# Cross-attentions of a twelve-layer kernel: flips handed over bank by bank, the output projection in the bank of the attended values, plain turns

## The chip, the cores and the metric

The kernel runs on one core of one Trainium2 chip, as one program that computes all twelve layers. The metric is the device time of a whole execution, in microseconds (us); lower is better.

## The reference, cut to what matters

The input `x` is 32 batches of 64 tokens with 256 channels. Twelve layers are added to it one after the other. Layers L0x, L2x and L3x are cross-attentions of 16 heads of 16 channels over 256 context tokens per batch:

```python
def _L0_xattn_ref(query, key, value, Wq, bq, Wk, bk, Wv, bv, Wo, bo):
    B, S, D, H = (4, 512, 256, 16)
    HD = D // H
    b = query.shape[0]
    Q = (query @ Wq + bq).reshape(b, -1, H, HD).transpose(0, 2, 1, 3)
    K = (key @ Wk + bk).reshape(b, -1, H, HD).transpose(0, 2, 1, 3)
    V = (value @ Wv + bv).reshape(b, -1, H, HD).transpose(0, 2, 1, 3)
    energy = jnp.einsum('bhqd,bhkd->bhqk', Q, K) / np.sqrt(HD)
    attn = jax.nn.softmax(energy, axis=-1)
    x = jnp.einsum('bhqk,bhkd->bhqd', attn, V)
    x = x.transpose(0, 2, 1, 3).reshape(b, -1, H * HD)
    return x @ Wo + bo
...
x = x + _L0_xattn_ref(_layernorm(x, axis=-1), ctx_1024, ctx_1024, ...)
```

L3x adds `mask * -1e9` to the scores. L2x has no projections at all: the normed `x` is the query, the context is key and value, and nothing is multiplied behind the attention. L0f is a layer whose two expert matrices are mixed anew for each of the 64 positions out of eight experts and then applied (`W1 = einsum('be,eoi->boi', g, eW1)`, a ReLU, and the same with `eW2`).

## The kernel before, in words

The three cross-attentions share `cross_attention` (line 739). `OWN` is true in L0x and L3x, where keys, values and output are projected, and false in L2x. Each engine runs its own list of instructions, written out by hand in a loop over the 32 batches `b`, and the engines meet by semaphores. The order of work on TensorE (PE) per batch is:

- `flip(b, 0)` (L924): eight transposes of the probabilities of the first half of the head pairs into `psT`, two PSUM banks. `PR` holds the probabilities, `PT` the transposed ones.
- `project_keys(b + 2)` (only OWN, L75 to L77 by way of `three_passes`) into the bank `psA`.
- `scores(b + 1, ...)` (L908, with a mask L912 too) into `psS`, four banks: both halves at once in the OWN layers, one half here and one half later in L2x.
- `flip(b, 1)`: eight more transposes into the same two banks.
- every second batch `finish(b // 2 - 1)`: the output projection of the last 128 tokens (L955), or in L2x two transposes (L957), into `psA`.
- in L2x the second half of the scores; in the OWN layers `project_values(b + 1)` into `psA`.
- `attend(b)`: two matmuls with `TWO`, the sum of two identities (L932), which turn the spread inverse sums `RB` around and add their two halves, into columns 128 to 255 of `psO`; then 32 matmuls (L944) of the probabilities with the values into columns 0 to 127 of `psO`.

ScalarE (ACT) takes the exponentials of a half (`exponentiate`, four ACTIVATEs with accumulation, L1001), copies bank 0 of `psT` to `PT` (`turned`, L1007), and in the OWN layers adds the key bias (`keys`, L1012) and rounds the context to its high part (`high`, L1019). Its order is `turned(b,0)`, `keys(b+2)`, `turned(b,1)`, both halves of `exponentiate(b+1)`, `high(b+4)`.

VectorE (DVE) takes the maxima (`largest`, L1044, 1,024 elements each), copies bank 1 of `psT` (`turned`, L1049), inverts the sums (`invert`, L1065), copies the values out of `psA` (`values`, L1053), scales the attended values (`attended`, L1071 and L1073), makes the low part of the context (`low`, L1058), and every second batch adds the projected output to `x` (`finish`, L1077). `turned(b,1)`, `finish`, `largest(b+1,1)`, `values(b+1)`, `attended(b)` follow one another in that order. GpSimd (POOL) spreads queries and inverse sums.

Two rules tie PE to the others. `psT` is handed over whole: `flip` waits until both copies of the flip before are done (`s_ta`, `s_td`), and signals once, behind its eighth transpose. And `psA` is shared: `FILLS` lists its users in order (K keys, W output projection, V values), and `claim` makes each wait until the one before has been read out (`s_empty`).

In L0f, `position_experts` (line 1700) runs 16 steps `k`. Its jobs go alternately to two sets of four PSUM banks, `S[0]` and `S[1]`, and `claim` makes a job wait until the job two places before it has been read out, by ACT, by DVE or by both. f0 to f3 and g0 to g3 are mixings (`mix2`, L1836, and `mix1`, L1823), which both engines read out; A0 and A1 apply the first mixed matrix (`apply1`, L1852 and L1859) and are read out by one ACT instruction; T turns the weights of the next block (L1810).

## Time and profile before

| what | value |
|---|---|
| median of three runs | 3020.52 us (3018.69 to 3025.06) |
| the profiled execution's own time | 3015.32 us |
| its span, first to last instruction | 3013.5 us |
| busy: PE, DVE, ACT, POOL | 86%, 60%, 45%, 21% |
| mean granted TensorE clock | 0.926 |
| batch loop of L0x | 59 to 322 us |
| 16 steps of L0f | 498 to 858 us |
| batch loop of L2x | 2036 to 2234 us |
| batch loop of L3x | 2531 to 2820 us |

The profile follows one execution. PE is matmul work, PEld the loading of the stationary operand, which runs ahead of the matmuls; of both, the start times are the best guide, since ends are modelled. A figure in square brackets behind a row is idle time of the engine just before it, with the instruction that ended it; "issue" is idle time for which the profile shows no releaser. A waiting share says little by itself: each loop has to be read for what closes it.

### The profile page before, as it was taken

What the parts mean: (1) busy time and instruction counts of PE and PEld (TensorE: products, weight loads), DVE (VectorE), ACT (ScalarE), POOL (GpSimd) and SP (SyncE); (2) the same over time, 40 slices, a digit from 0 to 9 for tenths busy, and PEclk for the clock granted to TensorE, in tenths of its full rate; (3) what the DMA queues carried; (4) which work ended last, traced back from release to release, by engine and by line L of the source; (5) the groups of instructions that cost most, each with busy time, mean ns of one, the idle gap of its engine ahead of it and who ended that gap; (6) DMA issues with size and microseconds to landing.
All of it is one profiled execution on the core that took longest, in us unless ns stands there. A gap on an engine that the chain in (4) does not pass through costs nothing. (4 is left out here: it accounts for less than half of the span.)

```text
span 3013.5 us, 83899 instructions
## 1 busy us (share of the span) xinstructions
PE 2583.9 (86%) x36083; PEld 2146.2 (71%) x36083; DVE 1794.8 (60%) x3365; ACT 1360.9 (45%) x3399; POOL 630.2 (21%) x752
## 2 busy tenths in 40 slices
PE   6999787999958999999987739959986767999888
PEld 5888555777747888888875539957764646888567
DVE  5777675666656444444445645657765866666663
ACT  3777324455532334444331314527763344666441
POOL 3111002211103111111102133422321423222200
PEclk9999898999979999999998559978998788999999
DMA  2110003211031000000000042332220001111100
GB/s 75 34 33 20 16 0 91 58 31 58 3 99 56 2 16 16 16 16 16 2 23 2 3 147 96 118 117 75 89 87 0 2 2 55 44 44 46 43 1 29
DMA packets 118221, 126.67 MB, mean 42 GB/s; under 512 B 10877, under 2 KB 110152, under 8 KB 117864
## 3 DMA queue, kind: packets, MB, share of 16 engines
q1 hardware_dynamic: 114024, 110.93, 11.8%
q0 software_dynamic: 3840, 10.49, 1.1%
q8 instruction: 284, 4.65, 0.6%
q14 instruction: 73, 0.60, 0.1%
HBM read 105.67 MB, written 15.73 MB: 40 GB/s over the span
## 5 line engine op out<-in xcount | busy, mean ns | idle before, releaser
L1001 ACT ACTIVATE s_ca_probs<-s_ca_scores,s_ca_neg_max 128x256 f32<-128x256 f32 x768 | 353.9, 483 | 12.8 <-DVE s_ca_neg_max L1044 9.8
L1044 DVE TENSOR_REDUCE s_ca_neg_max<-s_ca_scores 128x4 f32<-128x1024 f32 x192 | 234.2, 1221 | 103.5 <-PE s_ca_scores L912 54.4
L924 PE MATMUL s_ca_probs_flipped<-identity,s_ca_probs 128*128 128x128 f32 x1536 | 212.6, 282 | 16.0 <-ACT s_ca_probs L1001 9.8
L1375 DVE RECIPROCAL s_cc_inv_sums<-s_cc_sums 128x512 f32<-128x512 f32 x32 | 107.4, 3357 | 182.5 <-PE s_cc_out L1275 182.5
L924 PEld LDWEIGHTS s_ca_probs_flipped<-identity,s_ca_probs 128*128 128x128 f32 x1536 | 167.6, 143 | 59.0 <-ACT s_ca_probs L1001 26.7
L1989 DVE COPY s_mx_w_mixed<-s_mx_ps 128x512 f32<-128x512 f32 x256 | 163.7, 684 | 58.9 <-PE s_mx_ps L1836 43.6
L1007 ACT COPY s_ca_probsT<-s_ca_probs_flipped 128x512 f32<-128x512 f32 x192 | 114.9, 598 | 172.9 <-PE s_ca_probs_flipped L924 172.9
L1944 ACT COPY s_mx_w_mixed<-s_mx_ps 128x512 f32<-128x512 f32 x256 | 137.5, 589 | 114.0 <-PE s_mx_ps L1823 95.1
L1195 POOL TENSOR_TENSOR s_cc_probs_of_both<-s_cc_probsT 128x1024 f32<-128x1024 f32 x32 | 76.8, 2401 | 520.7 <-DVE s_cc_probsT L1366 520.7
L838 POOL TENSOR_TENSOR s_ca_inv_spread<-s_ca_inv_sums,h_ca_own_half 128x128 f32<-128x128 f32 x192 | 72.8, 401 | 473.7 <-DVE s_ca_inv_sums L1065 473.7
L1001 ACT ACTIVATION_READ_ACCUMULATOR s_ca_probs<-s_ca_scores,s_ca_neg_max 128x1 f32 x768 | 164.6, 214 | 0.0
L604 PE MATMUL s_ln_flip<-identity,s_ln_xn 128*128 128x128 f32 x352 | 65.4, 372 | 108.7 <-DVE s_ln_xn L586 108.5
L75 PE MATMUL s_cc_shared<-s_cc_ctxT_low,h_cc_wkv_high 128*128 128x256 f32 x512 | 147.9, 289 | 7.2 <-ACT s_cc_v L1337 3.8
L76 PE MATMUL s_cc_shared<-s_cc_ctxT_high,h_cc_wkv_low 128*128 128x256 f32 x512 | 144.6, 282 | 0.0
L77 PE MATMUL s_cc_shared<-s_cc_ctxT_high,h_cc_wkv_high 128*128 128x256 f32 x512 | 144.5, 282 | 0.0
L1049 DVE COPY s_ca_probsT<-s_ca_probs_flipped 128x512 f32<-128x512 f32 x192 | 131.4, 684 | 21.0 <-PE s_ca_probs_flipped L924 20.2
L604 PEld LDWEIGHTS s_ln_flip<-identity,s_ln_xn 128*128 128x128 f32 x352 | 62.1, 199 | 113.4 <-DVE s_ln_xn L586 112.4
L1327 ACT COPY s_cc_kT<-s_cc_shared 128x512 f32<-128x512 f32 x128 | 75.2, 587 | 90.0 <-PE s_cc_shared L77 88.8
L944 PE MATMUL s_ca_out<-s_ca_probsT,h_ca_v_spread 128*32 128x64 f32 x6144 | 106.5, 221 | 1.3 <-DVE s_ca_probsT L1049 1.3
L75 PEld LDWEIGHTS s_cc_shared<-s_cc_ctxT_low,h_cc_wkv_high 128*128 128x128 f32 x512 | 97.2, 190 | 14.6 <-ACT s_cc_v L1337 7.6
L75 PE MATMUL s_cc_shared<-h_cc_wkv_low,s_cc_ctxT_high 128*128 128x512 f32 x256 | 104.5, 408 | 1.7 <-issue 1.7
L1331 ACT ACTIVATE s_cc_probsT<-s_cc_scores 128x1024 f32<-128x1024 f32 x64 | 63.6, 1026 | 88.9 <-PE s_cc_scores L1257 88.5
(488 smaller groups left out, 7284.8 us busy)
## 6 DMA issues: line engine op xcount, KB each, us to landing
h_ca_ctxT<-in_ctxT SPq DMA_DIRECT2D x96, 256.0 KB, 3.2
h_mx_w_by_input<-in_L_ffn_eW1T SPq DMA_DIRECT2D x16, 512.0 KB, 5.1
h_mx_w_by_hidden<-in_L_ffn_eW2T SPq DMA_DIRECT2D x8, 1024.0 KB, 6.2
h_re_win<-in_L_ffn_W_in SPq DMA_DIRECT2D x8, 1024.0 KB, 5.9
h_ca_ctx<-in_ctx SPq DMA_DIRECT2D x32, 256.0 KB, 2.8
x_normed_transposed<-in_ctx SPq DMA_DIRECT2D x7, 1024.0 KB, 5.5
h_re_wout<-in_L_ffn_W_out SPq DMA_DIRECT2D x8, 512.0 KB, 3.8
choice_results<-s_rt_zeros SPq DMA_DIRECT2D x4, 1024.0 KB, 10.5
```

Of the source, the lines that this page charges most:

```text
L75: nc.tensor.matmul(dst, lhs[0], rhs[1], start=start, stop=False)
L76: nc.tensor.matmul(dst, lhs[1], rhs[0], start=False, stop=False)
L77: return nc.tensor.matmul(dst, lhs[0], rhs[0], start=False, stop=stop)
L604: last = nc.tensor.transpose(flip[u % 4][:, c, k, :], XN[:, t, c * P:(c + 1) * P], ident[:, :])
L924: last = nc.tensor.transpose(psT[:, 2 * a + c, :], PR[b % 2][:, 4 * n + a, c * P:(c + 1) * P], ident[:, :])
L1001: last = nc.scalar.activation(PR[b % 2][:, p, :], psS[:, p // 2, (p % 2) * NKEY:(p % 2 + 1) * NKEY], ACT.Exp, bias=nmax[b % 2][:, p:p + 1] ...
L1007: nc.scalar.copy(PT[b % 2][:, 4 * n:4 * n + 2, :, :].rearrange("p a c q -> p (a c) q"), psT[:, 0:4, :]).then_inc(s_ta, 1)
L1044: nc.vector.tensor_reduce(nmax[b % 2][:, 4 * n:4 * n + 4], psS[:, 2 * n:2 * n + 2, :].rearrange("p r (g k) -> p r g k", g=GR), AX_X, ALU.m ...
L1049: nc.vector.tensor_copy(PT[b % 2][:, 4 * n + 2:4 * n + 4, :, :].rearrange("p a c q -> p (a c) q"), psT[:, 4:8, :]).then_inc(s_td, 1)
L1375: nc.vector.reciprocal(RD[:, :, :], psD[:, :, :]).then_inc(s_rd, 1)
L1944: last = nc.scalar.copy(part(int(name[1]), r), bank(j, r))
L1989: last = nc.vector.tensor_copy(part(int(name[1]), r), bank(j, r))
```

## The change

- **Flips by bank.** `psT` becomes a list of separate banks, two in the OWN layers and three in L2x. Each flip is made of two groups of four transposes; group `u` goes to bank `u % len(psT)`, waits only until that bank's last reader has emptied it, and signals by itself. Even groups are read by ACT, odd ones by DVE. L2x gets its third bank because `psA` no longer exists there.
- **Output projection beside the attended values.** `finish` writes columns 128 to 383 of `psO` (`psW`) and no longer takes part in `FILLS`. So `project_values` doesn't wait for DVE to add the output to `x`; `attend` waits for it instead (`s_we`), every second batch.
- **Plain turns.** The two matmuls with `TWO` become two 128 x 128 transposes with the identity into columns 128 to 383 of `psO`, and the DVE copy of 128 columns becomes a reduction over pairs out of 256 columns. `TWO` and the instruction that made it go.
- **L0f.** A0 goes ahead of f1 on all three engines that handle it.

```diff
--- before.py
+++ after.py
@@ -749,11 +749,8 @@
     for b in range(NB):
...
-        if b and b % 2 == 0:
-            FILLS.append(("W", b // 2 - 1))
...
-    FILLS.append(("W", TILES - 1))
...
@@ -781,16 +777,18 @@
-        psT = ps("ca_probs_flipped", [P, 8, P])
-        psA = ps("ca_shared", [P, 512])
+        psT = [ps("ca_probs_flipped", [P, 4, P]) for _ in range(2 if OWN else 3)]
+        psA = ps("ca_shared", [P, 512]) if OWN else None
...
-        psA2 = psA[:, :].rearrange("p (a b) -> p a b", a=2)
+        psA2 = psA[:, :].rearrange("p (a b) -> p a b", a=2) if OWN else None
+        psW = psO[:, P:P + DIM]
...
+        s_wf, s_we = sem("output_ready"), sem("x_updated")
...
@@ -914,23 +912,27 @@
                 def flip(b, n):
-                    k = 2 * b + n
-                    pe.wait_ge(s_e, k + 1)
-                    if k:
-                        pe.wait_ge(s_ta, k)
-                        pe.wait_ge(s_td, k)
-                    for a in range(4):
-                        for c in range(2):
-                            last = nc.tensor.transpose(psT[:, 2 * a + c, :], PR[b % 2][:, 4 * n + a, c * P:(c + 1) * P], ident[:, :])
-                    last.then_inc(s_t, 1)
+                    pe.wait_ge(s_e, 2 * b + n + 1)
+                    for h in range(2):
+                        u = 4 * b + 2 * n + h
+                        was = u - len(psT)
+                        if was >= 0:
+                            pe.wait_ge(s_td if was % 2 else s_ta, was // 2 + 1)
+                        for a in range(2):
+                            for c in range(2):
+                                last = nc.tensor.transpose(psT[u % len(psT)][:, 2 * a + c, :],
+                                                           PR[b % 2][:, 4 * n + 2 * h + a, c * P:(c + 1) * P], ident[:, :])
+                        last.then_inc(s_t, 1)
...
                 def attend(b):
...
+                    if b and b % 2 == 0:
+                        pe.wait_ge(s_we, b // 2)
                     for g in range(GR):
-                        nc.tensor.matmul(psO[:, P + g * SEQ:P + (g + 1) * SEQ], RB[b % 2][:, g, :, :, :].rearrange("p r h d -> p (r h d)"),
-                                         TWO[:, :], start=True, stop=True)
+                        nc.tensor.transpose(psO[:, P + g * P:P + (g + 1) * P], RB[b % 2][:, g, :, :, :].rearrange("p r h d -> p (r h d)"),
+                                            ident[:, :])
...
@@ -948,14 +950,13 @@
                 def finish(i):
-                    claim(("W", i))
...
                     for g in range(GR):
...
-                            last = nc.tensor.matmul(psA[:, 0:DIM], AT[i % 2][:, g, :], WO[:, g, :], start=(g == 0), stop=(g == GR - 1))
+                            last = nc.tensor.matmul(psW, AT[i % 2][:, g, :], WO[:, g, :], start=(g == 0), stop=(g == GR - 1))
...
-                            last = nc.tensor.transpose(psA[:, g * P:(g + 1) * P], AT[i % 2][:, g, :], ident[:, :])
-                    last.then_inc(s_fill, 1)
+                            last = nc.tensor.transpose(psW[:, g * P:(g + 1) * P], AT[i % 2][:, g, :], ident[:, :])
+                    last.then_inc(s_wf, 1)
...
@@ -1003,8 +1002,9 @@
                 def turned(b, n):
-                    act.wait_ge(s_t, 2 * b + n + 1)
-                    nc.scalar.copy(PT[b % 2][:, 4 * n:4 * n + 2, :, :].rearrange("p a c q -> p (a c) q"), psT[:, 0:4, :]).then_inc(s_ta, 1)
+                    u = 4 * b + 2 * n
+                    act.wait_ge(s_t, u + 1)
+                    nc.scalar.copy(PT[b % 2][:, 4 * n:4 * n + 2, :, :].rearrange("p a c q -> p (a c) q"), psT[u % len(psT)][:, :, :]).then_inc(s_ta, 1)
...
@@ -1045,8 +1045,9 @@
                 def turned(b, n):
-                    dve.wait_ge(s_t, 2 * b + n + 1)
-                    nc.vector.tensor_copy(PT[b % 2][:, 4 * n + 2:4 * n + 4, :, :].rearrange("p a c q -> p (a c) q"), psT[:, 4:8, :]).then_inc(s_td, 1)
+                    u = 4 * b + 2 * n + 1
+                    dve.wait_ge(s_t, u + 1)
+                    nc.vector.tensor_copy(PT[b % 2][:, 4 * n + 2:4 * n + 4, :, :].rearrange("p a c q -> p (a c) q"), psT[u % len(psT)][:, :, :]).then_inc(s_td, 1)
...
@@ -1067,23 +1068,22 @@
                 def attended(b):
...
-                    halves = psO[:, 0:2 * P].rearrange("p (k g q) -> p k g q", k=2, g=GR)
-                    nc.vector.tensor_copy(RT[:, :, :], halves[:, 1]).then_inc(s_rt, 1)
+                    nc.vector.tensor_reduce(RT[:, :, :], psO[:, P:3 * P].rearrange("p (g h q) -> p g q h", g=GR, h=2), AX_X,
+                                            ALU.add).then_inc(s_rt, 1)
...
-                    nc.vector.tensor_tensor(at, halves[:, 0], RT[:, :, :], ALU.mult).then_inc(s_at, 1)
+                    nc.vector.tensor_tensor(at, psO[:, 0:P].rearrange("p (g q) -> p g q", g=GR), RT[:, :, :], ALU.mult).then_inc(s_at, 1)
...
                 def finish(i):
-                    dve.wait_ge(s_fill, PLACE[("W", i)] + 1)
-                    nc.vector.tensor_tensor(X[:, i, :], psA[:, 0:DIM], X[:, i, :], ALU.add).then_inc(s_empty, 1)
+                    dve.wait_ge(s_wf, i + 1)
+                    nc.vector.tensor_tensor(X[:, i, :], psW, X[:, i, :], ALU.add).then_inc(s_we, 1)
...
                 def statistics(i):
-                    dve.wait_ge(s_empty, PLACE[("W", i)] + 1)
+                    dve.wait_ge(s_we, i + 1)
...
@@ -1709,7 +1709,7 @@
-    ORDER = ("f0", "f1", "A0", "T", "f2", "A1", "f3", "FL", "g0", "Y0", "g1", "Y1", "g2", "g3")
+    ORDER = ("f0", "A0", "f1", "T", "f2", "A1", "f3", "FL", "g0", "Y0", "g1", "Y1", "g2", "g3")
...
@@ -1892,8 +1892,8 @@
                 for k in range(NK):
...
+                    apply1(k, 0)
...
-                    apply1(k, 0)
...
@@ -1960,8 +1960,8 @@
                 for k in range(NK):
...
+                    hidden(k, 0)
...
-                    hidden(k, 0)
```

PE in L0x, a batch with an output projection, from the scores to the start of the values; before:

```order
L908 MATMUL s_ca_scores<-s_ca_kT,s_ca_q_spread 128x256 [waits s4_probs_ready_1,s2_ln_normed_1,s2_ln_flipped_1]
L908 MATMUL s_ca_scores<-s_ca_kT,s_ca_q_spread 128x256 x7
L924 MATMUL s_ca_probs_flipped<-identity,s_ca_probs 128x128 [waits s4_probsT_by_dve_1,s4_probsT_by_act_1,s4_probs_ready_1]
L924 MATMUL s_ca_probs_flipped<-identity,s_ca_probs 128x128 x7
L955 MATMUL s_ca_shared<-h_ca_wo,s_ca_attendedT 128x256 [waits s4_attendedT_ready_1,s2_ln_normed_1]
L955 MATMUL s_ca_shared<-h_ca_wo,s_ca_attendedT 128x256
L75 MATMUL s_ca_shared<-h_ca_wkv_low,h_ca_ctxT_high 128x256 [waits s2_ln_normed_1]
L76 MATMUL s_ca_shared<-h_ca_wkv_high,h_ca_ctxT_low 128x256
```

and after the change:

```order
L906 MATMUL s_ca_scores<-s_ca_kT,s_ca_q_spread 128x256 [waits s4_probs_ready_1,s2_ln_normed_1,s2_ln_first_root_taken_1]
L906 MATMUL s_ca_scores<-s_ca_kT,s_ca_q_spread 128x256 x7
L923 MATMUL s_ca_probs_flipped<-identity,s_ca_probs 128x128 [waits s4_probsT_by_act_1,s4_probs_ready_1]
L923 MATMUL s_ca_probs_flipped<-identity,s_ca_probs 128x128 x3
L923 MATMUL s_ca_probs_flipped<-identity,s_ca_probs 128x128 [waits s4_probsT_by_dve_1]
L923 MATMUL s_ca_probs_flipped<-identity,s_ca_probs 128x128 x3
L956 MATMUL s_ca_out<-h_ca_wo,s_ca_attendedT 128x256 [waits s4_attendedT_ready_1]
L956 MATMUL s_ca_out<-h_ca_wo,s_ca_attendedT 128x256
L75 MATMUL s_ca_shared<-h_ca_wkv_low,h_ca_ctxT_high 128x256 [waits s2_ln_normed_1]
L76 MATMUL s_ca_shared<-h_ca_wkv_high,h_ca_ctxT_low 128x256
```

The flip is cut in two groups with one wait on each copying engine, and the output projection has moved from the shared bank to `s_ca_out` and lost its wait on the bank; the wait of the values ahead of L75 now is for the keys' readout alone.

PE in L2x (no projections), a batch with `finish`, from the second flip to the turns of the inverse sums; before:

```order
L924 MATMUL s_ca_probs_flipped<-identity,s_ca_probs 128x128 [waits s21_probsT_by_dve_2,s21_probsT_by_act_2,s21_probs_ready_2]
L924 MATMUL s_ca_probs_flipped<-identity,s_ca_probs 128x128 x7
L957 MATMUL s_ca_shared<-identity,s_ca_attendedT 128x128 [waits s21_attendedT_ready_5,s19_choices5_loaded_1]
L957 MATMUL s_ca_shared<-identity,s_ca_attendedT 128x128
L908 MATMUL s_ca_scores<-h_ca_ctxT,s_ca_q_spread 128x256 [waits s21_probs_ready_2,s16_rstds_ready_1,s19_choices6_loaded_1]
L908 MATMUL s_ca_scores<-h_ca_ctxT,s_ca_q_spread 128x256 x3
L932 MATMUL s_ca_out<-s_ca_two_identities,s_ca_inv_spread 128x64 [waits s21_attendedT_ready_5,s21_inv_sums_spread_2]
L932 MATMUL s_ca_out<-s_ca_two_identities,s_ca_inv_spread 128x64
L944 MATMUL s_ca_out<-s_ca_probsT,h_ca_v_spread 32x64 [waits s21_probsT_by_dve_2,s21_probsT_by_act_2,s17_ln_stored_6]
L944 MATMUL s_ca_out<-s_ca_probsT,h_ca_v_spread 32x64 x31
```

and after (the name of a semaphore in brackets is that of its first user, since semaphores are reused):

```order
L923 MATMUL s_ca_probs_flipped<-identity,s_ca_probs 128x128 [waits s21_probsT_by_dve_2,s21_probs_ready_2]
L923 MATMUL s_ca_probs_flipped<-identity,s_ca_probs 128x128 x3
L923 MATMUL s_ca_probs_flipped<-identity,s_ca_probs 128x128 [waits s21_probsT_by_act_2]
L923 MATMUL s_ca_probs_flipped<-identity,s_ca_probs 128x128 x3
L958 MATMUL s_ca_out<-identity,s_ca_attendedT 128x128 [waits s21_attendedT_ready_5]
L958 MATMUL s_ca_out<-identity,s_ca_attendedT 128x128
L906 MATMUL s_ca_scores<-h_ca_ctxT,s_ca_q_spread 128x256 [waits s21_probs_ready_2,s16_attendedT_ready_4,s19_x_updated_5]
L906 MATMUL s_ca_scores<-h_ca_ctxT,s_ca_q_spread 128x256 x3
L934 MATMUL s_ca_out<-identity,s_ca_inv_spread 128x128 [waits s19_choices7_loaded_1,s21_attendedT_ready_5,s21_inv_sums_spread_2]
L934 MATMUL s_ca_out<-identity,s_ca_inv_spread 128x128
```

The second flip's first group waits for DVE's last copy and the exponentials, its second group for ACT's copy; the turns carry a new wait, that for the update of `x` (shown under a reused name).

PE in L0f, from the last mixing of `g` to the turning of the next weights; before:

```order
L1836 MATMUL s_mx_ps<-me_gate_blocks,s_mx_w_2 128x128 [waits s2_ln_flipped_1,s2_ln_stored_1]
L1836 MATMUL s_mx_ps<-me_gate_blocks,s_mx_w_2 128x128 x15
L1836 MATMUL s_mx_ps<-me_gate_blocks,s_mx_w_2 128x128 [waits s2_ln_stored_1,s2_ln_flipped_1]
L1836 MATMUL s_mx_ps<-me_gate_blocks,s_mx_w_2 128x128 x15
L1852 MATMUL s_mx_ps<-h_mx_b_1,me_gate_rows 128x128 [waits s2_ln_flipped_1,s2_ln_stored_1]
L1852 MATMUL s_mx_ps<-h_mx_b_1,me_gate_rows 128x128 x3
L1859 MATMUL s_mx_ps<-s_mx_w_mixed,x_normed_transposed 32x128 x32
L1810 MATMUL s_mx_ps<-identity,h_mx_w_expert_last 128x128 [waits s2_ln_scales_ready_1,s2_ln_stored_1,s2_ln_flipped_1]
L1810 MATMUL s_mx_ps<-identity,h_mx_w_expert_last 128x128 x15
L1836 MATMUL s_mx_ps<-me_gate_blocks,s_mx_w_2 128x128 [waits s2_ln_flipped_1]
```

and after:

```order
L1823 MATMUL s_mx_ps<-me_gate_blocks,s_mx_w_1 128x128 [waits s2_ln_stored_1]
L1823 MATMUL s_mx_ps<-me_gate_blocks,s_mx_w_1 128x128 x15
L1836 MATMUL s_mx_ps<-me_gate_blocks,s_mx_w_2 128x128 [waits s2_ln_flipped_1,s2_ln_stored_1]
L1836 MATMUL s_mx_ps<-me_gate_blocks,s_mx_w_2 128x128 x15
L1852 MATMUL s_mx_ps<-h_mx_b_1,me_gate_rows 128x128 [waits s2_ln_flipped_1,s2_ln_stored_1]
L1852 MATMUL s_mx_ps<-h_mx_b_1,me_gate_rows 128x128 x3
L1859 MATMUL s_mx_ps<-s_mx_w_mixed,x_normed_transposed 32x128 x32
L1836 MATMUL s_mx_ps<-me_gate_blocks,s_mx_w_2 128x128 [waits s2_ln_stored_1,s2_ln_flipped_1]
L1836 MATMUL s_mx_ps<-me_gate_blocks,s_mx_w_2 128x128 x15
L1810 MATMUL s_mx_ps<-identity,h_mx_w_expert_last 128x128 [waits s2_ln_scales_ready_1,s2_ln_flipped_1]
```

A0 (L1852, L1859) has moved ahead of the second L1836 job, and the turning now waits for what A0 filled.

## Rows read from the trace of the kernel before

**Rows 1.** The page, part 1: busy time, share, instructions.

```profile
PE 2583.9 (86%) x36083; PEld 2146.2 (71%) x36083; DVE 1794.8 (60%) x3365; ACT 1360.9 (45%) x3399; POOL 630.2 (21%) x752
```

**Rows 2.** Waits of PEld, L0x (first) and L3x: total us, times, longest.

```profile
PEld s_ca_shared L75 <- DVE x_resident L1077: 13.9, 15, 1.0
...
PEld s_ca_shared L75 <- DVE x_resident L1077: 13.8, 15, 1.0
```

**Rows 3.** Timeline of L0x, PEld: start, length, engine, line, operation, idle before.

```profile
150.60 0.85 PEld L924 LDWEIGHTS s_ca_probs_flipped<-identity,s_ca_probs 128*128 128x128 f32 x8
...
158.00 0.86 PEld L924 LDWEIGHTS s_ca_probs_flipped<-identity,s_ca_probs 128*128 128x128 f32 x8
...
161.53 0.86 PEld L924 LDWEIGHTS s_ca_probs_flipped<-identity,s_ca_probs 128*128 128x128 f32 x8 [0.33 <-issue]
...
162.35 0.73 PEld L955 LDWEIGHTS s_ca_shared<-h_ca_wo,s_ca_attendedT 128*128 128x128 f32 x4
...
165.43 0.54 PEld L932 LDWEIGHTS s_ca_out<-s_ca_two_identities,s_ca_inv_spread 128*128 128x128 f32 x4
...
166.03 0.94 PEld L944 LDWEIGHTS s_ca_out<-s_ca_probsT,h_ca_v_spread 128*32 128x32 f32 x64
```

**Rows 4.** Timeline of L0x, ACT, DVE and the values' first load.

```profile
155.74 0.48 ACT L1001 ACTIVATE s_ca_probs<-s_ca_scores,s_ca_neg_max 128x256 f32<-128x256 f32 x1
...
159.35 0.67 ACT L1019 CAST h_ca_ctxT_high<-h_ca_ctxT 128x512 fp32r<-128x512 f32 x1
...
161.67 1.23 DVE L1044 TENSOR_REDUCE s_ca_neg_max<-s_ca_scores 128x4 f32<-128x1024 f32 x1 [0.22 <-PE s_ca_scores L908]
...
163.53 0.42 DVE L1077 TENSOR_TENSOR x_resident<-s_ca_shared,x_resident 128x256 f32<-128x256 f32 x1
...
164.01 0.19 PEld L75 LDWEIGHTS s_ca_shared<-h_ca_wkv_low,h_ca_ctxT_high 128*128 128x128 f32 x1 [0.92 <-DVE x_resident L1077]
```

**Rows 5.** Timeline of L2x: PEld, DVE and ACT around two batches.

```profile
2101.42 0.52 PEld L932 LDWEIGHTS s_ca_out<-s_ca_two_identities,s_ca_inv_spread 128*128 128x128 f32 x4 [0.33 <-issue]
...
2106.10 0.25 PEld L957 LDWEIGHTS s_ca_shared<-identity,s_ca_attendedT 128*128 128x128 f32 x2
...
2106.52 0.73 PEld L908 LDWEIGHTS s_ca_scores<-h_ca_ctxT,s_ca_q_spread 32*128 32x128 f32 x8 [0.17 <-POOL s_ca_q_spread L828]
...
2107.02 0.41 DVE L1077 TENSOR_TENSOR x_resident<-s_ca_shared,x_resident 128x256 f32<-128x256 f32 x1
...
2107.58 0.52 PEld L932 LDWEIGHTS s_ca_out<-s_ca_two_identities,s_ca_inv_spread 128*128 128x128 f32 x4 [0.33 <-issue]
...
2110.78 0.60 ACT L1007 COPY s_ca_probsT<-s_ca_probs_flipped 128x512 f32<-128x512 f32 x1
...
2111.44 0.86 PEld L924 LDWEIGHTS s_ca_probs_flipped<-identity,s_ca_probs 128*128 128x128 f32 x8 [0.49 <-ACT s_ca_probs L1001]
...
2113.53 0.52 PEld L932 LDWEIGHTS s_ca_out<-s_ca_two_identities,s_ca_inv_spread 128*128 128x128 f32 x4 [0.33 <-issue]
...
2113.65 1.22 DVE L1044 TENSOR_REDUCE s_ca_neg_max<-s_ca_scores 128x4 f32<-128x1024 f32 x1 [0.38 <-PE s_ca_scores L908]
```

**Rows 6.** L2x's start: windows (five engines, clock, DMA share, GB/s), then timeline.

```profile
2040.00:2050.00 10.00, 10.00 (x102) 7.56 (x102) 4.35 (x8) 4.77 (x19) 2.07 (x5) 0.54 0.00 0
2050.00:2060.00 10.00, 9.89 (x147) 7.60 (x151) 8.10 (x13) 7.30 (x27) 3.40 (x8) 1.00 0.32 108
...
2041.68 1.57 PEld L924 LDWEIGHTS s_ca_probs_flipped<-identity,s_ca_probs 128*128 128x128 f32 x8 [0.65 <-issue]
```

**Rows 7.** Timeline of L0f, PEld: f0, f1, A0, T.

```profile
643.86 1.01 PEld L1836 LDWEIGHTS s_mx_ps<-me_gate_blocks,s_mx_w 32*128 32x128 f32 x32 [0.23 <-issue]
...
645.29 1.01 PEld L1836 LDWEIGHTS s_mx_ps<-me_gate_blocks,s_mx_w 32*128 32x128 f32 x32 [0.42 <-ACT s_mx_w_mixed L1944]
...
646.48 0.34 PEld L1852 LDWEIGHTS s_mx_ps<-h_mx_b,me_gate_rows 8*128 8x128 f32 x8 [0.17 <-issue]
...
648.83 1.73 PEld L1810 LDWEIGHTS s_mx_ps<-identity,h_mx_w_expert_last 128*128 128x128 f32 x16 [0.20 <-issue]
```

8 lines of the change are left out of this document (2 added, 6 removed).

## The prediction

> **What bounds the kernel now.** I read the page first: PE is busy 86% of the span [rows 1], but that is an average, so I went to the three batch loops and asked in each what closes it. In the timelines the starts of the PEld rows are the thing to follow, and the figures in brackets.
>
> L0x and L3x are bound by PE's own list. From one first flip to the next a batch without output projection takes 7.40 us (150.60 to 158.00), and in it PE never waits for another engine; the one gap is 0.33 us of "issue" between scores and flip [rows 3]. Every second batch has the output projection, and there PE does wait: behind L955 it stands 0.92 us until DVE has added the result to `x`, because the values share its bank [rows 4]. That wait occurs 15 times in each of the two layers, 13.9 and 13.8 us in all [rows 2].
>
> L2x is another loop. ACT finishes the exponentials, copies bank 0 (0.60 us), and only then may the next flip start, at 2111.44, 0.66 us behind the copy's start; the maximum of the scores behind it starts at 2113.65, and the next exponentials wait for it or for ACT's second copy [rows 5]. A batch takes 6.16 us with `finish` (2101.42 to 2107.58) and 5.95 without (to 2113.53). PE is nearly as long: of the 0.49 us it waits ahead of the flip, 0.33 would stand anyway, as the same step from scores to a full-height operation shows ahead of L932. So without waits PE needs 5.95 - 0.16 = 5.79 and, with `finish`, 6.00 us [rows 5].
>
> **The change part by part.**
>
> *Output projection beside the attended values.* It removes the 0.92 us waits: 13.9 + 13.8 = 27.7 us [rows 2]. What is late next? The values then wait for the keys' readout alone, which ACT made long before. L955 itself stays on the path. In its old place it followed the flip with no gap (161.53 + 0.86 against 162.35) although a wait stands on it [rows 3]; I take none behind it either. The new wait stands ahead of the turns in `attend`, and the 32 matmuls of the attended values are queued behind it. In L0x DVE's addition ended at 163.95 [rows 4]; the values need 165.43 - 164.01 = 1.42 us, so with the wait gone the turns start 165.43 - 0.92 = 164.51, 0.56 us later than the addition's end [rows 3, 4]. Cost zero. The addition could slip by 0.5 us before that cover is gone, and then each microsecond more costs 15 us per layer.
>
> *Plain turns.* L932 has four weight loads for its two matmuls and holds PE 0.60 us (165.43 to 166.03) [rows 3]. The nearest operation to the new one is L957, two transposes with the identity: 0.25 us of loads, and 0.42 us until the scores behind it start [rows 5]. The last 0.17 is a gap before an operation of another shape; ahead of L944 the old gap was 0.06. So the new turns take 0.31 to 0.42 us, and they save 0.18 to 0.29. I take 0.18, since a 128-column transpose is what stands ahead of that gap in both cases. For 64 batches of L0x and L3x that is 11.5 us (to 18.6). L2x's share is below. The reduction of 256 PSUM elements in place of the 128-element copy costs DVE at most the 0.42 us of an addition of 256 elements [rows 4], at a place where DVE next waits for the flip; nothing on the path. The Trainium skill (TensorE: Matmul & The Clock Gate, Terms) calls transpose mode four times faster for FP32. Taken literally that would make 0.54 us of loads 0.14 and the saving 0.40, 14 us more over 64 batches. L957's two loads already take 0.25 here [rows 5], so the measurement decides against it.
>
> *Flips by bank, OWN layers.* The two copies no longer wait for each other, and ACT can start four transposes earlier: 0.43 us, half of the flip's 0.86 [rows 3]. PE isn't waiting for them there, so this is worth nothing. It adds a wait in the middle of 63 flips in each of L0x, L2x and L3x, 189 in all. A satisfied wait within operations of one shape had no gap (flip to L955, above) [rows 3], and three waits with a change of shape ahead of L944 had 0.06 [rows 3]: 0 to 11 us. I take 0, for the shape doesn't change.
>
> *The other loop in L0x.* When PE gets faster, the next limit is softmax and context splitting: exponentials 155.74 to 159.35 (3.61 us), then high part, low part, DVE's copy and inversion until the maximum could start, 161.67 - 0.22 - 159.35 = 2.10, the maximum 1.23, and some 0.05 to the exponentials: 6.99 us [rows 4]. PE then needs 7.40 - 0.18 = 7.22. That still holds, by 0.23 us. L3x has its mask matmuls on PE and more room.
>
> *Three banks in L2x.* The second flip's first group no longer waits for ACT's copy; only its second group does. So the ring shrinks by four transposes, 0.43: to 5.52 and 5.73 us. PE's own list shrinks only by the turns' 0.18: to 5.61 and 5.82. PE is the longer. In the `finish` batches there is a new delay: the addition ended 0.15 us ahead of the turns before (2107.02 + 0.41 against 2107.58), and now the scores behind the flip, and so the turns, come up to 0.4 us earlier, while the addition stays behind DVE's maximum and copy [rows 5]. I put 0.15 us on those batches (0 to 0.3). Sum for two batches: 12.11 - (5.61 + 5.97) = 0.53, times 16 = 8.5 us. The start of this layer runs at the lower clock level, 0.54 in 2040 to 2050 us, where a flip's loads take 1.57 us and not 0.86 [rows 6]; those two batches give back about twice as much, 1 us more. So 9.5 us (7 to 12).
>
> *L0f.* f1 waited 0.42 us for the set that g3 had filled, then A0 came 1.19 us later and took 2.35 us to T (643.86, 645.29, 646.48, 648.83) [rows 7]. Now A0 makes that same wait, f1 follows 2.35 us later and finds its set empty, and needs 1.01 us of loads plus a change of shape. So 1.19 becomes 1.01 to 1.19; I take 0.1 us less per step, 14 steps with a T: 1.4 us (0 to 2.5).
>
> *The rest.* `TWO` goes, one short DVE instruction per layer ahead of the loop; the reduction adds some 0.1 us at each layer's end: zero together, give or take 1 us.
>
> **The sum.** 27.7 + 11.5 + 0 + 9.5 + 1.4 = 50.1 us off the span of 3013.5. The profiled execution itself took 3015.3, 5.2 us under the median of 3020.5; I take the gain off both alike: its own time 2965, the median 2970.
>
> **Rivals.**
> - *The loop behind takes over.* ACT and DVE in L0x need 6.99 by the rows against PE's 7.22. If the two slow each other by 0.3 us, L0x gains nothing from the turns (5.8 us), and if L2x's addition waits longer, 3 us more: 2979. For it: the room is only 3%. Against: in every second batch PE has 0.73 us of L955 besides [rows 3], which lets them catch up.
> - *Small waits add up.* 189 x 0.06 = 11 us for the handover inside flips: 2982.
> - *The third bank does nothing,* because something else keeps the second flip: 9.5 us missing, 2980. Against it: the flip starts 0.06 us behind ACT's copy in the batch shown [rows 5].
> - *Slower: each handover stops the array.* If the wait between the two groups, with the signal behind the fourth transpose, made PE run empty as it does between scores and flip (0.33 us [rows 3]), 189 of them would cost 62 us: 2970 + 62 = 3032. It decides from 0.27 us per handover on. Against: flip to L955 with a wait has no gap at all [rows 3].
> - *Slower: the clock of L2x stays low.* L2x starts at 0.54 and is at full level from the next window [rows 6]. There a batch costs 1.57/0.86 as much, 11 us and not 6; if it stayed so, 30 batches would add some 150 us: 3120. PE was filled without a break of its own before the rise, and the change leaves it as full. The Trainium skill (TensorE: Matmul & The Clock Gate, Part 4: PE-mode transpose) says that transposes don't count as PE being busy for the clock gate, and this change turns matmuls into transposes. In L2x they are two of 58 matmul instructions per batch, beside 16 transposes that were there before.
>
> **How the numbers follow.** Forecast (2960 to 2977, from the bounds of the terms): 0.70. Still faster, under 2960 (turns at 0.29, shorter PE in L2x): 0.08. Gain of 15 to 43 us by one of the first three rivals: 0.15. Within 0.2%, about 6 us and what a measurement of this kernel can tell from no change: 0.02. Slower: handover 0.03, clock 0.02. The likeliest is 2970. The range 2957 to 2986 leaves out the two slower cases, no change, and half of the tails. Faster 0.93, same 0.02, slower 0.05.
>
> **What would show it.** PEld's wait for DVE's addition is gone in L0x and L3x, and L75 follows L955 at once. L0x's batches take about 7.2 and 7.95 us, L3x's follow. The turns hold PE 0.4 us. L2x's batches alternate around 5.6 and 5.9, ACT's second copy follows its first without 1.2 us of idle time, and the `finish` batch may show a short wait for the addition ahead of the turns. In L0f T comes about 4.9 us behind f0. What would make it wrong: gaps between the two groups of a flip, DVE's maxima ending later than PE's scores allow in L0x, or a longer low-clock stretch at 2030 us.

## The result, and the profile after

| what | before | after |
|---|---|---|
| median | 3020.35 us (3018.69 to 3025.06) | 2975.83 us (2971.5 to 2980.13) |
| ratio | | 0.9848, 95% interval 0.9832 to 0.9863 |
| the profiled execution's own time, span | 3015.32, 3013.5 us | 2971.50, 2969.7 us |

Forecast were 2970 us (2960 to 2977 the likeliest stretch) and a gain of 50.1; measured are 44.5 us between the medians and 43.8 between the spans. One trace among the experiments below, the first of two_banks, comes from an execution of 3774.81 us with a mean granted clock of 0.63, and no reading rests on it. To see where the 43.8 us came from I took, in both traces, the start of the first and of the last batch's attended values (PEld, `s_ca_out<-s_ca_probsT`, L944 before and L946 after) in each cross-attention, and the first and the last flip of the hidden values (L1868) in L0f. Between these marks:

| stretch | before, us | after, us | gained | forecast |
|---|---|---|---|---|
| start to first mark of L0x | 67.17 | 66.55 | 0.6 | |
| L0x, from batch 1 to batch 32 | 251.17 | 233.56 | 17.6 | 19.6 |
| to L0f | 192.54 | 188.95 | 3.6 | 0 |
| L0f, first to last of 16 steps | 340.60 | 342.76 | -2.2 | 1.4 |
| to L2x | 1195.16 | 1194.24 | 0.9 | 0 |
| L2x, from batch 1 to batch 32 | 187.81 | 178.05 | 9.8 | 9.5 |
| to L3x | 307.10 | 307.16 | -0.1 | 0 |
| L3x, from batch 1 to batch 32 | 277.17 | 259.66 | 17.5 | 19.6 |
| to the end | 194.78 | 198.78 | -4.0 | 0 |

The three loops gave 44.9 us, L0f took 2.2 back, and the stretches between the loops, whose code is nearly all the same in both kernels, moved by up to +3.6 and -4.0. I don't count these as effects of the change, since one and the same kernel scatters as much: the two traces of the changed kernel with the old order of L0f (l0f_back and l0f_back_2 below) have 187.66 and 195.18 us from L0x to L0f and 198.79 and 195.10 in the last stretch, and the two traces of the changed kernel 1194.24 and 1212.46 from L0f to L2x. Over all traces of this study the stretch ahead of L0x is 66.5 to 70.3 us, that from L0x to L0f 187.6 to 195.2, that from L0f to L2x 1193.3 to 1212.6, that from L2x to L3x 300.7 to 307.9, and the last 194.8 to 198.8, while batch loops of the same code repeat to 0.6 us (with one exception, in l0f_only below). The last stretch after the change, its windows first and then those of before (columns: length, busy time of PE, PEld, DVE, ACT and POOL, granted clock, DMA share, GB/s):

```profile
2842.00:2852.00 10.00, 6.03 (x29) 6.00 (x30) 6.95 (x25) 5.31 (x9) 0.10 (x1) 0.50 0.00 0
2852.00:2862.00 10.00, 6.26 (x18) 4.80 (x18) 5.32 (x14) 7.32 (x18) 0.00 (x0) 0.67 0.01 2
```

```profile
2890.00:2900.00 10.00, 5.58 (x32) 5.32 (x32) 6.10 (x19) 6.39 (x14) 0.00 (x0) 0.71 0.01 2
2900.00:2910.00 10.00, 8.73 (x31) 7.06 (x32) 7.85 (x17) 8.11 (x18) 0.00 (x0) 0.83 0.00 0
```

At the same place of the code, some 71 us behind the last mark of L3x, the first windows have PE busy 6.03 and 5.58 us in ten, and the clock stood at its lower level (0.50) in one execution and at 0.71 in the mean in the other. So single traces are compared by loops here, not by spans.

**L0x after** (timeline, as in [rows 3, 4]), a batch with output projection:

```profile
154.97 0.86 PEld L923 LDWEIGHTS s_ca_probs_flipped<-identity,s_ca_probs 128*128 128x128 f32 x8 [0.33 <-issue]
...
155.80 0.73 PEld L956 LDWEIGHTS s_ca_out<-h_ca_wo,s_ca_attendedT 128*128 128x128 f32 x4
...
156.56 0.19 PEld L75 LDWEIGHTS s_ca_shared<-h_ca_wkv_low,h_ca_ctxT_high 128*128 128x128 f32 x1
156.58 0.47 PE L75 MATMUL s_ca_shared<-h_ca_wkv_low,h_ca_ctxT_high 128*128 128x256 f32 x1
...
156.77 0.19 PEld L76 LDWEIGHTS s_ca_shared<-h_ca_wkv_high,h_ca_ctxT_low 128*128 128x128 f32 x1
...
156.97 0.42 DVE L1078 TENSOR_TENSOR x_resident<-s_ca_out,x_resident 128x256 f32<-128x256 f32 x1
...
158.09 0.25 PEld L934 LDWEIGHTS s_ca_out<-identity,s_ca_inv_spread 128*128 128x128 f32 x2
158.51 0.94 PEld L946 LDWEIGHTS s_ca_out<-s_ca_probsT,h_ca_v_spread 128*32 128x32 f32 x64 [0.17 <-issue]
```

The 0.92 us of waiting ahead of L75 [rows 4] are gone, the addition ends at 157.39, 0.70 us ahead of the turns that wait for it, and the turns hold PE from 158.09 to 158.51, 0.42 us, with the forecast gap of 0.17. New is what stands behind L75: the next load comes 0.21 us later and not 0.11 as before:

```profile
164.12 0.19 PEld L76 LDWEIGHTS s_ca_shared<-h_ca_wkv_high,h_ca_ctxT_low 128*128 128x128 f32 x1
```

The values take 158.09 - 156.56 = 1.53 us instead of 1.42.

**L2x after** (as in [rows 5]), the second flip and the turns of a `finish` batch, then the turns of the next:

```profile
2081.73 0.60 ACT L1007 COPY s_ca_probsT<-s_ca_probs_flipped 128x512 f32<-128x512 f32 x1
...
2082.02 0.86 PEld L923 LDWEIGHTS s_ca_probs_flipped<-identity,s_ca_probs 128*128 128x128 f32 x8 [0.33 <-ACT s_ca_probs L1000]
...
2082.72 0.59 ACT L1007 COPY s_ca_probsT<-s_ca_probs_flipped 128x512 f32<-128x512 f32 x1 [0.39 <-PE s_ca_probs_flipped L923]
...
2083.88 0.41 DVE L1078 TENSOR_TENSOR x_resident<-s_ca_out,x_resident 128x256 f32<-128x256 f32 x1
...
2084.41 0.20 PEld L934 LDWEIGHTS s_ca_out<-identity,s_ca_inv_spread 128*128 128x128 f32 x2 [0.41 <-issue]
...
2089.98 0.20 PEld L934 LDWEIGHTS s_ca_out<-identity,s_ca_inv_spread 128*128 128x128 f32 x2 [0.33 <-issue]
```

The second flip starts 0.29 us behind the start of ACT's copy, before that copy has ended; before it was 0.66 us. PE's gaps are now those of its own list, but for one: 0.41 and not 0.33 ahead of the turns of the `finish` batch, where the addition ends at 2084.29. Batches take 5.57 and 5.87 us. The turns are a little cheaper here than in L0x: 0.37 us from their first load to that of L946 (2084.41 to 2084.78) where the two matmuls took 0.59 (2107.58 to 2108.17). The layer ran at a granted clock of 0.53 in 2020 to 2030 us and at 1.00 in the next window, as before. The Trainium skill (TensorE: Matmul & The Clock Gate, Part 4: PE-mode transpose) says that a transpose doesn't count as PE being busy in the same way. This case can't refute it; it shows that with 18 and not 16 transposes among the 58 matmul instructions of a batch the clock rose all the same and stayed at 1.00.

**L0f after** (as in [rows 7]), first an inner step, then one of the last two, which have no T:

```profile
558.80 0.76 PEld L1836 LDWEIGHTS s_mx_ps<-me_gate_blocks,s_mx_w 32*128 32x128 f32 x24 [0.20 <-issue]
...
560.07 0.31 PEld L1836 LDWEIGHTS s_mx_ps<-me_gate_blocks,s_mx_w 32*128 32x128 f32 x8 [0.51 <-issue]
560.50 1.73 PEld L1810 LDWEIGHTS s_mx_ps<-identity,h_mx_w_expert_last 128*128 128x128 f32 x16
...
805.39 1.88 PEld L1836 LDWEIGHTS s_mx_ps<-me_gate_blocks,s_mx_w 32*128 32x128 f32 x64 [0.20 <-issue]
...
808.04 0.34 PEld L1852 LDWEIGHTS s_mx_ps<-h_mx_b,me_gate_rows 8*128 8x128 f32 x8 [0.77 <-ACT s_mx_w_mixed L1944]
```

Two things were not forecast. Inside f1, between its 24th and 25th load, the row of loads has a hole of 0.51 us for which the profile shows no releaser. And where T is missing, f1 and f2 follow each other (x64), and A1 waits 0.77 us until ACT has read f1 out. In the old order A0 lay between them and A1 did not wait, as the same place before shows:

```profile
827.39 0.98 PEld L1836 LDWEIGHTS s_mx_ps<-me_gate_blocks,s_mx_w 32*128 32x128 f32 x32 [0.20 <-issue]
828.27 0.32 PEld L1852 LDWEIGHTS s_mx_ps<-h_mx_b,me_gate_rows 8*128 8x128 f32 x8
```

### The profile page after: what moved, and what is told of

Read it like the earlier page. It is cut to its first block and busy times, and to the rows that moved or that the text cites. A ratio compares the mean times of both kernels' runs of the same rounds, so it can differ in the third digit from the quotient of the medians.

```text
span 2969.7 us, 83477 instructions
## 1 busy us (share of the span) xinstructions
PE 2556.6 (86%) x35891; PEld 2119.0 (71%) x35891; DVE 1806.7 (61%) x3362; ACT 1368.2 (46%) x3399; POOL 629.7 (21%) x752
## 5 line engine op out<-in xcount | busy, mean ns | idle before, releaser
L923 PE MATMUL s_ca_probs_flipped<-identity,s_ca_probs 128*128 128x128 f32 x1536 | 213.8, 283 | 11.5 <-ACT s_ca_probs L1000 10.6
L75 PE MATMUL s_cc_shared<-s_cc_ctxT_low,h_cc_wkv_high 128*128 128x256 f32 x512 | 147.9, 289 | 7.2 <-ACT s_cc_v L1337 3.8
L75 PEld LDWEIGHTS s_cc_shared<-s_cc_ctxT_low,h_cc_wkv_high 128*128 128x128 f32 x512 | 97.2, 190 | 14.6 <-ACT s_cc_v L1337 7.6
L946 PE MATMUL s_ca_out<-s_ca_probsT,h_ca_v_spread 128*32 128x64 f32 x6144 | 106.5, 221 | 1.0 <-DVE s_ca_probsT L1050 1.0
L75 PE MATMUL s_cc_shared<-h_cc_wkv_low,s_cc_ctxT_high 128*128 128x512 f32 x256 | 104.5, 408 | 0.0
## 6 DMA issues: line engine op xcount, KB each, us to landing
choice_results<-s_rt_zeros SPq DMA_DIRECT2D x4, 1024.0 KB, 10.5
```

What stands on the lines that cost most here:

```text
L75: nc.tensor.matmul(dst, lhs[0], rhs[1], start=start, stop=False)
L923: last = nc.tensor.transpose(psT[u % len(psT)][:, 2 * a + c, :], PR[b % 2][:, 4 * n + 2 * h + a, c * P:(c + 1) * P], ident[:, :])
```

## The experiments

All were read by the same marks, each from one trace. Loops in us; "plain / W" is a batch without and with output projection (in L2x without and with `finish`).

| kernel | L0x | plain / W | L2x | plain / W | L3x | plain / W | L0f |
|---|---|---|---|---|---|---|---|
| before | 251.17 | 7.41 / 9.06 | 187.81 | 5.95 / 6.16 | 277.17 | 8.28 / 9.92 | 340.60 |
| projection_only | 239.21 | 7.41 / 8.27 | 187.83 | 5.95 / 6.16 | 265.30 | 8.28 / 9.13 | 344.29 |
| turns_only | 247.36 | 7.23 / 8.97 | 187.61 | 5.94 / 6.15 | 272.10 | 8.11 / 9.75 | 340.35 |
| whole_handover | 235.74 | 7.24 / 8.20 | 177.58 | 5.57 / 5.87 | 260.27 | 8.11 / 8.96 | 346.96 |
| two_banks_2 | 233.56 | 7.23 / 8.09 | 189.77 | 5.99 / 6.21 | 259.66 | 8.11 / 8.96 | 342.57 |
| finish_first | 234.53 | 7.24 / 8.14 | 177.91 | 5.57 / 5.87 | 260.82 | 8.11 / 9.02 | 342.84 |
| after | 233.56 | 7.23 / 8.09 | 178.05 | 5.57 / 5.87 | 259.66 | 8.11 / 8.96 | 342.76 |
| after_again | 233.56 | 7.23 / 8.09 | 177.90 | 5.57 / 5.87 | 259.67 | 8.11 / 8.96 | 343.23 |

**The output projection alone** (`psW = psO[:, P:P + DIM]` in L0x and L3x, with its own two semaphores, all else as before):

```diff
-        if b and b % 2 == 0:
+        if not OWN and b and b % 2 == 0:
             FILLS.append(("W", b // 2 - 1))
...
+                    if OWN and b and b % 2 == 0:
+                        pe.wait_ge(s_we, b // 2)
...
-                            last = nc.tensor.matmul(psA[:, 0:DIM], AT[i % 2][:, g, :], WO[:, g, :], start=(g == 0), stop=(g == GR - 1))
+                            last = nc.tensor.matmul(psW, AT[i % 2][:, g, :], WO[:, g, :], start=(g == 0), stop=(g == GR - 1))
```

> The kernel before with only the output projection of L0x and L3x moved beside the attended values (own semaphores, no place in the shared bank; the turns with the sum of two identities, whole flips, L2x and L0f as before). The prediction's term: both waits go, 27.7 us: 2992.7. My theory from the changed kernel's trace: behind the projection the first matmul of the values takes 0.47 us and the next starts 0.31 us behind it, where the old wait hid that change from one kind of matmul to the other; so 0.11 to 0.13 us in 30 batches come back, 3.3 to 3.9 us: 2996.4.

Measured: 2998.83 us against 3025.07 of before on the same chip, ratio 0.991 (0.989 to 0.9929). The loops lost 11.96 and 11.87 us, 23.8 together: the second value, not 27.7. A W batch costs 0.86 us more than a plain one where the loads of the projection alone are 0.73.

**Plain turns alone** (the two transposes and DVE's reduction, all else as before):

```diff
-                        nc.tensor.matmul(psO[:, P + g * SEQ:P + (g + 1) * SEQ], RB[b % 2][:, g, :, :, :].rearrange("p r h d -> p (r h d)"),
-                                         TWO[:, :], start=True, stop=True)
+                        nc.tensor.transpose(psO[:, P + g * P:P + (g + 1) * P], RB[b % 2][:, g, :, :, :].rearrange("p r h d -> p (r h d)"),
+                                            ident[:, :])
...
```

> The kernel before with only the plain turns and the reduction of DVE. The prediction's term: 0.18 us in each of 64 batches of L0x and L3x, nothing in L2x, where the ring closes each batch: 3020.4 - 11.5 = 3008.9. Rival: the turns save in L2x as well, 32 x 0.18 = 5.8 more: 3003.1. Second rival: in the batches with an output projection the longer DVE step (0.42 us instead of 0.29) delays the addition to x that the values wait for, by up to 0.13 us 30 times: 3012.8.

Measured: 3015.68 us, ratio 0.997 (0.9956 to 0.9983). Plain batches gained 0.18 and 0.17 us, as forecast, and L2x 0.2 us in all, so its ring (exponentials, ACT's copy, flip, maximum) did hide the turns. A W batch of L0x gained only 0.09: what it waits for is DVE's addition, and that did not come earlier by as much. The last two intervals of each layer gained next to nothing (in L0x 8.25 to 8.23 us, then 4.91 both times). Loops: 3.8 + 5.1 = 8.9 us.

**Whole flips in L0x and L3x** (the changed kernel; one wait for both copies ahead, one signal behind):

```diff
-                        if was >= 0:
+                        if OWN and h == 0 and was >= 0:
+                            pe.wait_ge(s_ta, 2 * b + n)
+                            pe.wait_ge(s_td, 2 * b + n)
+                        if not OWN and was >= 0:
                             pe.wait_ge(s_td if was % 2 else s_ta, was // 2 + 1)
...
-                        last.then_inc(s_t, 1)
+                        if not OWN:
+                            last.then_inc(s_t, 1)
+                    if OWN:
+                        last.then_inc(s_t, 2)
```

> The changed kernel with whole flips again in L0x and L3x: both copies are waited for ahead of the first transpose, and one signal of two stands behind the eighth; nothing inside the flip. The prediction's zero: batches stay at 7.23, 8.09, 8.11 and 8.96 us. If the wait and signal inside each of 126 flips cost PE something, the batches get shorter by it twice (0.06 each would be 7.11 and 7.99). If the handover by bank had gained anything in these layers, they get longer.

Measured: 2992.21 us in a single run. Plain batches stay at 7.24 and 8.11: a wait and a signal in the middle of a flip cost PE nothing. But the W batches of L0x got 0.11 us longer. Timeline of this kernel, such a batch:

```profile
157.97 0.69 DVE L1065 TENSOR_TENSOR h_ca_ctxT_low<-h_ca_ctxT,h_ca_ctxT_high 128x512 fp32r<-128x512 f32 x1 [1.32 <-ACT h_ca_ctxT_high L1025]
...
158.58 0.68 DVE L1056 COPY s_ca_probsT<-s_ca_probs_flipped 128x512 f32<-128x512 f32 x1
...
159.38 0.86 PEld L926 LDWEIGHTS s_ca_probs_flipped<-identity,s_ca_probs 128*128 128x128 f32 x8 [0.43 <-issue]
```

DVE's copy ends at 159.26, and the second flip, which must have it, starts at 159.38, 0.43 us behind the scores' loads and not 0.33. The profile puts this down to "issue"; that the gap is 0.10 longer than at the same place elsewhere, and ends just behind the copy, speaks for the copy. In the changed kernel only the second half of that flip needs DVE's copy. Handover by bank is thus worth 2.2 us in L0x and 0.6 in L3x. In each layer 0.6 of it lies in the last two intervals. There no scores stand between the two flips, and the second one waited for the copies of the first in the kernel before too; timeline of before, the last batch of L0x:

```profile
314.46 0.86 PEld L924 LDWEIGHTS s_ca_probs_flipped<-identity,s_ca_probs 128*128 128x128 f32 x8
...
316.39 0.86 PEld L924 LDWEIGHTS s_ca_probs_flipped<-identity,s_ca_probs 128*128 128x128 f32 x8 [1.08 <-issue]
```

After the change that gap is 0.68 us.

**Two banks in L2x** (`for _ in range(2)` in place of three in the changed kernel). It was run twice, and the loop is read from the trace of the second.

> The changed kernel with two banks of flipped probabilities in L2x instead of three; all else as changed. By the prediction's ring (exponentials, ACT's copy, flip, maximum) L2x falls back to batches of 5.95 and 6.16 us, since the turns' saving lies beside that ring: 2975.8 + 9.8 = 2985.6. The rival 'the third bank does nothing': 2975.8, and L2x stays at 178 us for its 31 batches. If the turns count even with two banks (TensorE and not the ring bounds L2x), 5.5 us of the 9.8 stay: 2980.

> The kernel with two banks in L2x once more, for a trace at the ordinary clock. By the ring of the prediction L2x returns to batches of 5.95 and 6.16 us, 187.8 us for its loop. If the third bank did nothing: 5.57 and 5.87, 178.0 us.

Measured: 2988.72 us, ratio 0.9873 (0.9856 to 0.9891) against 0.9848 of the changed kernel, and 2994.38 us in the second, a single run. The loop went back to 189.77 us. The third bank carries the whole gain of L2x and 2 us more; with two banks the rest of the change makes this layer 2 us slower than it was, batches of 5.99 and 6.21 us where 5.95 and 6.16 were expected. Timeline of two_banks_2:

```profile
2122.34 0.60 ACT L1007 COPY s_ca_probsT<-s_ca_probs_flipped 128x512 f32<-128x512 f32 x1
2123.05 0.86 PEld L923 LDWEIGHTS s_ca_probs_flipped<-identity,s_ca_probs 128*128 128x128 f32 x8 [0.75 <-ACT s_ca_probs L1000]
```

This is the ring of the prediction: the flip waits for the copy's end. It starts 0.71 us behind the copy's start where it was 0.66 before [rows 5]; these 0.05 us a batch make most of the 2 us, and which part of the change brings them no run separates.

**The projection ahead of the second flip** (changed kernel, L0x and L3x; on DVE the addition ahead of the second copy):

```diff
-                    flip(b, 1)
-                    if b and b % 2 == 0:
+                    if OWN and b and b % 2 == 0:
                         finish(b // 2 - 1)
+                    flip(b, 1)
+                    if not OWN and b and b % 2 == 0:
+                        finish(b // 2 - 1)
```

> The changed kernel with the output projection of L0x and L3x ahead of the second flip instead of behind it (on DVE the addition to x goes ahead of its second copy). Theory 'change of kind': the 0.13 us that a batch with output projection costs beyond its 0.73 us of loads arises because the projection stands directly ahead of the values' matmuls of another kind; ahead of the transposes, whose kind is the same, it goes: 8.09 to 7.96 us in L0x, 8.96 to 8.83 in L3x, 30 x 0.13 = 3.9 us less than the changed kernel. Rival: the 0.13 belongs to the projection wherever it stands (its own fill and drain): no difference. Second rival: the flip comes 0.73 us later, so do ACT's second copy and all the exponentials, and the loop behind (6.99 us by my sum of before) closes the batches: slower.

Measured: 2987.21 us, ratio 0.9837 (0.9813 to 0.9861), beside 0.9826 for the changed kernel in the same group, which is the same within the intervals. The loops got longer by 1.0 and 1.2 us. My theory of a change of kind falls:

```profile
156.27 0.73 PEld L956 LDWEIGHTS s_ca_out<-h_ca_wo,s_ca_attendedT 128*128 128x128 f32 x4 [0.33 <-issue]
157.02 1.01 PEld L923 LDWEIGHTS s_ca_probs_flipped<-identity,s_ca_probs 128*128 128x128 f32 x8
158.00 0.19 PEld L75 LDWEIGHTS s_ca_shared<-h_ca_wkv_low,h_ca_ctxT_high 128*128 128x128 f32 x1
```

Now the flip follows the projection, and its eight loads take 1.01 us and not 0.86. So the price doesn't come with the change of kind: in both places, what stands behind the projection pays 0.1 to 0.15 us. The likeliest reason is that the projection's loads end before its matmuls do, as the row of its matmuls in the kernel before says, 1.03 us beside 0.73 of loads [rows 3] (ends of PE rows are modelled, so the size of this tail isn't measured):

```profile
162.46 1.03 PE L955 MATMUL s_ca_shared<-h_ca_wo,s_ca_attendedT 128*128 128x256 f32 x4
```

**The changed kernel again.**

> The changed kernel once more, unaltered, as the common measure of this group and for a second trace. The batch loops should repeat to 0.1 us: 233.6, 178.0 and 259.7 us from the first to the last batch's attended values. If the long steps of L0f come with its new order, they come back as often as in the first trace (four gaps of 0.30 to 0.71 us inside f1, 342.8 us from first to last flip of the hidden values); if they are an accident of an execution, their number and place differ, and without them the steps give 339.2 us (340.6 before, less 14 x 0.1).

Measured: 2986.90 us against 3035.24 of before on that chip, ratio 0.9826 (0.9802 to 0.9851). The loops repeat to 0.15 us. L0f has five gaps: 0.23 with 8 loads of f1 left, 0.43 with 21, 0.53 with 4, at the places of the first trace, one of 1.06 behind 17 loads of f0, where the first had 0.66, and one of 0.49 ahead of the last load of f3 in the fifth step, where the first had none. The places belong to the program, not to the execution; how long a gap is, and whether one is seen at such a place, varies. (Of the four that I had put inside f1, three are; the fourth is in f0.)

**The order of L0f.** The old order in the changed kernel (twice) and the new order in the kernel before:

```diff
-    ORDER = ("f0", "A0", "f1", "T", "f2", "A1", "f3", "FL", "g0", "Y0", "g1", "Y1", "g2", "g3")
+    ORDER = ("f0", "f1", "A0", "T", "f2", "A1", "f3", "FL", "g0", "Y0", "g1", "Y1", "g2", "g3")
...
```

> The changed kernel with only the order of L0f undone (f0, f1, A0, T again on all three engines). The prediction's term says that the new order saves 0.1 us in 14 steps, so this kernel would be 1.4 us slower than the changed one: 2977.2. My theory from the trace of the changed kernel: f1 now stands right behind A0's 72 short operations with no wait between, and TensorE runs out of instructions in the middle of f1 in some steps (gaps of 0.30 to 0.71 us, put down to 'issue', four of them), so the order costs 2.2 us net and this kernel takes 2973.6, with 16 steps in 340.6 us and no gap inside f1. If the long steps were an accident of that one execution, the term stands and it is 2977.2.

> The kernel with the changed cross-attentions and the old order of L0f, once more, for a second trace. The first had a stretch of lowered clock in its second step (30.23 us, 2.4 us over the usual), so its 343.6 us were 341.1 without that. I expect 340.4 to 341.3 us from first to last flip, 2 us less than with the new order, and the batch loops of the changed kernel: 233.6, 177.9 and 259.7 us. If the new order's term of the prediction holds, 340.6 and the new order's clean steps would differ the other way.

> The kernel before with only the new order of L0f. If the cost belongs to the order, this trace shows what five traces of kernels with it showed: gaps inside f1 in the steps at about 50, 205 and 230 us behind the first flip of the hidden values, and the two last steps, which have no T, at 20.3 us each and not 19.7 and 19.8; 342.6 to 343.2 us from first to last flip. If it came from the cross-attentions (by where their code ends, or by the clock that they leave), it shows 340.6 less 1.4: 339.2 us, and the last steps at 19.7.

Measured: 2983.51 us, ratio 0.9864 (0.9848 to 0.988), then 2976.34 and 3031.66 in single runs (before 3023.58 beside them). Times of whole runs don't resolve 2 us here. The whole of L0f took 343.55 and 343.23 us with the old order in the changed kernel, which is no less than with the new one and more than the 340.4 to 341.3 that I expected of the second, and 343.95 with the new order in the kernel before, for which I had 342.6 to 343.2. All three have one step disturbed by something else, so the steps have to be read one by one. In some executions one or two of the first two steps take 2.3 to 2.6 us more, in a window of lowered clock (0.89 in the mean of 31 us in l0f_back), whatever the order. Without it the two traces of the old order are at 341.1 and 340.9. The steps 3 to 13 and the last two are free of it:

| kernel | order | steps 3 to 13, best step of each parity | their sum beyond that | last two |
|---|---|---|---|---|
| before, turns_only | old | 22.31, 22.23 | 0.4, 0.1 | 39.5, 39.5 |
| projection_only | old | 22.31, 22.23 | 1.3 | 39.6 |
| l0f_back, l0f_back_2 | old | 22.32, 22.23 | 0.9, 0.6 | 39.5, 39.5 |
| after, after_again | new | 22.19, 22.15 (22.12) | 2.8, 3.2 | 40.6, 40.6 |
| two_banks_2, finish_first, whole_handover | new | 22.19, 22.12 | 2.6, 2.8, 1.9 | 40.6 |
| l0f_only | new | 22.19, 22.15 | 0.7 | 41.5 |
| code_shift | new | 22.19, 22.15 | 2.0 | 40.8 |
| t_first | T ahead of f1 | 22.29, 22.24 | 0.4 | 40.9 |

(Two steps in a row belong to one block of weights and differ a little, so each of the two has its own best time. The sum beyond is the 11 steps less six times the first and five times the second figure, taken as 22.32 and 22.23 for the old order, 22.19 and 22.15 for the new.) The clean inner step did get 0.1 us shorter, 1.2 us in eleven, and the first two give 0.2 more. The last two lost 1.15 by the A1 wait shown above, in every kernel with the new order; that was missed. And gaps took 0.7 to 3.2 us where the old order had 0.1 to 1.3. l0f_only has none at the three places inside f1 where I expected them; it has one of 0.37 elsewhere and two of 0.66 and 0.63 in its last step. The old order has gaps too, inside A0; l0f_back_2, and l0f_back at the same 16 loads and with the same 0.56:

```profile
723.97 1.25 PEld L1859 LDWEIGHTS s_mx_ps<-s_mx_w_mixed,x_normed_transposed 128*32 128x32 f32 x48
725.78 0.43 PEld L1859 LDWEIGHTS s_mx_ps<-s_mx_w_mixed,x_normed_transposed 128*32 128x32 f32 x16 [0.56 <-issue]
```

**What the gaps are.** Two kernels: five more transposes of the identity on PE ahead of the first g0, and T ahead of f1.

```diff
                 pe.wait_ge(s_b, 128)
+                first = claim(job(0, "g0"))
+                for j in range(5):
+                    nc.tensor.transpose(first[:, 0, 0:P], ident[:, :], ident[:, :])
```

> The changed kernel with five more transposes of the identity on TensorE ahead of the first mixing g0 of L0f (into a bank that g0 overwrites); they cost some 0.6 us once. They shift every later instruction of TensorE by five places in its list. If the gaps inside f1 arise where the supply of instructions is renewed, at fixed places of the list, each moves five matmuls (ten loads) ahead in its job: with 18 loads left and not 8, 31 and not 21, 14 and not 4. If they belong to what f1 reads or to other engines, they stay where they were.

> The changed kernel with T ahead of f1 in L0f: f0, A0, T, f1, f2. If it is the stretch of short operations (72 of A0, then 32 of f1, at 0.03 us each) that empties the supply of instructions, T's 16 long ones (1.73 us) in between let it catch up, and no gap inside f1 is left. But f1 and f2 then stand side by side, and A1 must wait for the readout of f1: f2's 1.0 us covers only part of its 1.3 us, so a step takes some 0.3 to 0.5 us more than the clean 22.17: 22.5 to 22.7, and the last two stay at 20.3. If the gaps are there as before, the stretch is not their cause.

Measured: 2979.79 and 2982.86 us, both in single runs. With the list shifted, the three gaps inside f1 are gone from their places, one inside f3 is new, and the one inside f0, in the fourth step, came 5 loads earlier (behind 17 loads, then behind 12). The job has 32 loads; those missing at the end of the rows are mixed with the first of A0. First the changed kernel, then code_shift:

```profile
577.77 0.63 PEld L1836 LDWEIGHTS s_mx_ps<-me_gate_blocks,s_mx_w 32*128 32x128 f32 x17 [0.23 <-issue]
579.05 0.42 PEld L1836 LDWEIGHTS s_mx_ps<-me_gate_blocks,s_mx_w 32*128 32x128 f32 x12 [0.66 <-issue]
```

```profile
587.07 0.55 PEld L1836 LDWEIGHTS s_mx_ps<-me_gate_blocks,s_mx_w 32*128 32x128 f32 x12 [0.23 <-issue]
588.63 0.64 PEld L1836 LDWEIGHTS s_mx_ps<-me_gate_blocks,s_mx_w 32*128 32x128 f32 x18 [1.01 <-issue]
```

I had written ten loads, wrongly: a transpose is one load with one matmul, a matmul in this type two, so five transposes shift by five loads, which this gap did. With T between A0 and f1 one visible gap was left, 0.26 us inside f3, and the clean step is 22.29 and 22.24, less than the 22.5 to 22.7 I expected.

What settles the place is a count over all traces. Number PE's instructions in the order of the trace, every load, every matmul and every semaphore instruction, counted from 0 at the first of the program. The 13 traces that are read here hold 29 gaps of 0.2 us and more inside a job of L0f for which no releaser is shown, in 11 of the traces, with either order of L0f and either kind of cross-attention. Divided by 256, the numbers of the instructions behind these gaps leave 69 or 70, all 29 of them. The gap in f0 stands at number 14149 in the changed kernel and at 14150 in code_shift, where five transposes (ten instructions) and one wait stand ahead and the same number falls five loads earlier into the job. So the gaps stand at every 256th instruction of PE's list or not at all; of the 58 such places in L0f a trace shows 0 to 5. Which jobs these places fall into changes with every instruction added ahead or moved, and that may be why the changed kernel has more gaps than l0f_only; no run tests it. It looks like a supply of instructions that is renewed there and sometimes comes late, but that is argued: no row shows the supply, nor why one place has a gap and another none.

**The rival of the low clock, seen by accident.** l0f_only has L2x as before, yet its loop took 198.27 us. Its windows at the start of the layer:

```profile
2055.00:2065.00 10.00, 10.00 (x100) 7.66 (x98) 4.42 (x7) 4.94 (x18) 1.53 (x4) 0.50 0.09 29
2065.00:2075.00 10.00, 10.00 (x99) 7.82 (x98) 4.50 (x8) 4.36 (x17) 2.07 (x5) 0.50 0.13 41
```

The layer stood at the lower level (0.50) for two more batches (10.73 and 11.15 us) although PE was busy all the time, then it rose; 10 us in one execution, without any edit to this layer. It is the price that I had put on a batch at that level. This run took 3031.66 us, 8 us over the run of before beside it.

## Why the prediction was right, and where not

The forecast gain was 5.6 us above the measured one, by terms that missed to both sides: output projection, turns and L0f gave 10.5 us less than forecast, flips by bank and L2x 3.1 more. That these partly cancel is luck; what closes each loop was read rightly in nearly all batches.

- *Output projection, 27.7:* measured 23.8 alone. The wait is gone in both layers, nothing waits for the addition instead, and the values follow L956 at once; that was right. The term was mis-sized by one reading: I took the projection to cost its 0.73 us of loads and found no gap ahead of it, but did not ask what it costs the work behind it. That is 0.13 us a batch, and it had lain inside the 0.92 us of waiting. 30 x 0.13 = 3.9. So W batches of L0x take 8.09 us and not 7.95. That it is the tail of the matmuls is the likeliest reason, not a measured one.
- *Plain turns, 11.5:* 8.9 alone, and behind the projection 235.74 and 260.27 against 239.21 and 265.30, so 3.5 + 5.0 = 8.5. The lower bound of 0.18 was right, it holds in every plain batch. W batches of L0x gave only 0.07, because DVE was late by 0.1 there, the last two intervals of each layer gave nothing, and the term counts 64 batches where the marks span 62.
- *That lateness is the first rival,* the loop behind. I gave it 0.23 us of room in plain batches and held that W batches have more. It was the other way round: with whole flips, DVE's low part and copy come 0.1 us too late for the second flip there. The rival's mechanism was there, at 0.11 us in 14 batches, 1.5 us and not 5.8, and the handover by bank took it away again.
- *Flips by bank in the OWN layers, 0:* worth 2.8 us. 1.6 of it is that it frees half of the flip from that late copy: "PE isn't waiting for them there" was true of these batches in the kernel before, and no longer with the other edits in. The other 1.2 lies in the last two intervals of the two layers, where the sentence was wrong from the start: the last second flip waited 1.08 us. The 126 waits in L0x and L3x cost nothing, as taken, so the rivals "small waits add up" and "stops the array" are out there; the 63 in L2x weren't tested by themselves.
- *L2x, 9.5:* measured 9.8. Batches of 5.57 and 5.87 against 5.61 and 5.97: the turns save 0.22 here and not 0.18, and the wait for the addition is 0.08 us (0.41 less 0.33) where I put 0.15. That makes 10 us behind the first batch, where I had 8.5. The 1 us more for the start at the lower clock is not there between the marks: the first interval is 6.95 us before and 7.08 and 6.93 in the two traces after. So the closeness of 9.8 to 9.5 is partly luck.
- *L0f, 1.4:* measured -2.2. The step that failed is "14 steps with a T": the two without one were left out, and they lose 1.15. The other part, gaps of 0.7 to 3.2 us at fixed places of PE's list, no row of before pointed to. The other 13 steps gained 1.4 without their gaps, as forecast.
- *Sum:* 23.8 + 8.5 + 2.8 + 9.8 - 2.2 = 42.7. The rest of the 43.8 is the balance of the stretches outside the loops, which scatter by more than that, the 0.6 ahead of L0x too.

With the old order of L0f the changed kernel should be 2 us faster by these steps. The two ratios, 0.9864 against 0.9848 and 0.9826, can't show that, so it is a reading of the steps, not a measured better version. And these 2 us are the gaps: without them the new order is 0.2 us ahead (1.4 less 1.15), and any instruction added ahead of L0f moves them.

## What to carry to other kernels

A wait that is removed hid things: what the operation ahead of it costs its successor, and an engine that was late by less than the wait. Read the PE row beside the PEld row before calling an operation as long as its loads. When jobs are reordered around two alternating buffers, go through the steps in which a job is missing too, and through the first and last batches of a loop. And several edits in one loop have to be costed in the state that the others leave: here more than half of what the handover by bank paid was there only because the other two had made PE faster.

## What the runs showed of the hardware

- A wait that is already met and a signal, between equal operations on PE, cost nothing that can be seen in 126 places (7.23 against 7.24 us a batch).
- Two 128-column transposes have 0.25 us of loads (0.20 in L2x) and 0.17 of gap ahead of 32-column matmuls, where the two matmuls with 64 moving columns had 0.54 and 0.06. From 32-row scores to the 128-row flips and turns the gap is 0.33. The Trainium skill (TensorEngine Tiling (Array Packing), Key Properties) says that a change of the tiling mode drains the array; the traces agree in that each such change named here has a gap, and they don't show the draining itself.
- PE's loads can have a hole of 0.2 to 1.1 us in the middle of a job of equal short operations with no wait on it. All 29 such gaps in L0f stand at the same place modulo 256 in PE's list of instructions (remainder 69 or 70), in 11 traces.
- A 31 us stretch with a mean clock of 0.89 may fall into one execution's L0f and not into the next one's: 2.4 us that have nothing to do with an edit.
